# Shared-key attention in a four-layer kernel: maxima scores with 48 rows a head, two heads at once in the array's rows, and a new home for the parts of each chunk

## The reference, cut to what matters

```
q = x @ Wq            # 16 heads of 16
k, v = x @ Wk, x @ Wv # one head of 16 each, shared by all query heads
s = q k^T / 4, masked to keys at or before the query
out = softmax(s) v, heads side by side, @ Wo + bo
```

## Time and profile before

| | us |
|---|---|
| median of 3 runs (1975.9 to 1980.74) | 1979.59 |
| the profiled execution's own time | 1982.36 |
| span of its trace | 1980.3 |
| PE busy, DVE busy, ACT busy, POOL busy | 1726.5, 1056.2, 754.8, 472.2 |
| units' reductions, line 1154 (x320) | 329.9 |
| exponentials, line 1040 (x640) | 318.0 |
| scores, line 917 (x640) | 209.5 |
| units' matmuls, line 892 (x640) | 184.1 |

### The profile page before, as it was taken

The page is one execution under the profiler, slowest core; times in us unless marked ns, Lnnn a source line. Parts: engine busy times, 40 slices in busy tenths (PEclk is TensorE's granted clock), DMA queues, the critical chain, the costliest instruction groups (busy, mean ns, idle before and its releaser), DMA issues.

```text
span 1980.3 us, 24253 instructions
## 1 busy us (share of the span) xinstructions
PE 1726.5 (87%) x9372; PEld 1022.2 (52%) x9372; DVE 1056.2 (53%) x1727; ACT 754.8 (38%) x1751; POOL 472.2 (24%) x474
## 2 busy tenths in 40 slices
PE   5899577889999999969997857896899999987998
PEld 3565444433343333534555433664677777773556
DVE  2666665557678776242222867242566666743222
ACT  1210023465676777621111121013666666651110
POOL 3753230110100000040000005741344444420000
PEclk9999786899999999979998978997899999997999
DMA  3000022000000000200001030000000000002000
GB/s 104 1 1 1 14 64 70 2 1 1 2 1 1 1 1 2 90 0 0 1 0 56 0 108 0 0 0 5 6 1 7 1 7 1 1 3 86 11 11 22
DMA packets 27410, 34.02 MB, mean 17 GB/s; under 512 B 5280, under 2 KB 24544, under 8 KB 26784
## 3 DMA queue, kind: packets, MB, share of 16 engines
q1 hardware_dynamic: 27296, 32.47, 5.3%
HBM read 22.86 MB, written 2.10 MB: 13 GB/s over the span
## 4 chain that ended last, share of the span: by engine, by line
PE 67%; DVE 14%; POOL 7%; issue 6%; ACT 3%; DMA 1%; SPq 1%; POOLq 0%; DVEq 0%; ACTq 0%
PE PS L930 6%; PE PS L1208 6%; PE PS L917 6%; PE PS L1214 6%; PE PS L892 5%; PE PS L1227 5%; PE PS L1994 3%; PE PS L357 3%; PE PS L1983 2%; PE PS L1961 2%; PE PS L1633 2%; POOL arena L2179 2%; DVE arena L1154 2%; PE PS L1614 2%; PE PS L967 2%
## 5 line engine op out<-in xcount | busy, mean ns | idle before, releaser
L1154 DVE TENSOR_REDUCE arena<-PS 128x1 f32<-128x1024 f32 (+7 forms) x320 | 329.9, 1060 | 136.4 <-PE PS L894 98.9
L1040 ACT ACTIVATE arena<-PS 128x512 f32<-128x512 f32 (+3 forms) x640 | 318.0, 534 | 168.6 <-PE PS L920 77.1
L917 PE MATMUL PS<-arena 99*128 99x512 bf16 (+3 forms) x640 | 209.5, 358 | 2.0 <-ACT arena L1040 1.5
L892 PE MATMUL PS<-arena 96*128 96x512 bf16 (+3 forms) x640 | 184.1, 366 | 24.7 <-DVE arena L1154 21.9
L190 POOL TENSOR_TENSOR rstd<-ve,mhalf 128x4 f32<-128x4 f32 x32 | 32.3, 1009 | 610.3 <-DVE ve L216 610.3
L930 PE MATMUL PS<-arena 128*32 128x512 f32 (+3 forms) x1280 | 155.7, 559 | 2.8 <-ACT arena L1046 1.7
L185 ACT ACTIVATE XT<-PS 128x1024 f32<-128x1024 f32 x36 | 36.8, 1024 | 313.5 <-PE PS L178 313.5
L917 PEld LDWEIGHTS PS<-arena 99*128 99x128 bf16 x640 | 61.3, 100 | 155.4 <-ACT arena L1040 112.9
L1208 PE MATMUL PS<-XT,arena 128*128 128x512 f32 x256 | 122.7, 602 | 14.9 <-DVE arena L2376 10.4
L1258 DVE TENSOR_TENSOR arena<-arena,PS 128x512 f32<-128x512 f32 x64 | 43.9, 686 | 164.3 <-PE PS L1214 164.1
L1243 ACT ACTIVATE arena<-PS 128x512 f32<-128x512 f32 x64 | 38.2, 597 | 232.7 <-PE PS L1208 232.7
(11 more groups left out here) (233 smaller groups left out, 3031.8 us busy)
## 6 DMA issues: line engine op xcount, KB each, us to landing
arena<-arena SPq DMA_DIRECT2D x55, 128.0 KB, 2.4
X<-in_L_attn_x SPq DMA_DIRECT2D x4, 512.0 KB, 5.4
arena<-in_L_attn_out_w SPq DMA_DIRECT2D x1, 2048.0 KB, 8.1
out<-X SPq DMA_DIRECT2D x4, 512.0 KB, 2.9
arena<-in_dmask SPq DMA_DIRECT2D x1, 1024.0 KB, 7.2
arena<-in_L_ffn_W_up SPq DMA_DIRECT2D x1, 1024.0 KB, 5.0
arena<-in_L_ffn_W_gate SPq DMA_DIRECT2D x1, 1024.0 KB, 7.4
arena<-in_L_ffn_W_down SPq DMA_DIRECT2D x1, 1024.0 KB, 9.0
```

The source lines that it names most:

```text
L892: last = pe.matmul(flat[:, o:o + w], q, a.KS[0:SROWS, CH * kc:CH * kc + w], start=True, stop=kc < c)
L917: last = pe.matmul(PS[:, b, lo:CH], a.KS[0:rows, P * j:P * (j + 1)], a.QS[0:rows, G1 * g + r, CH * c + lo:CH * (c + 1)], start=True, stop= ...
L1040: act.activation(a.PB[:, n % 3, r, lo:CH], PS[:, 4 + x % 3, lo:CH], ACT.Exp, scale=D0 ** -0.5).then_inc(a.e2, 1)
L1154: dve.tensor_reduce(dst, src, AX.X, ALU.max, negate=True).then_inc(a.m1, 1)
```

## The change

The maxima no longer come from six products of parts but from three (high x high, middle x high, high x middle): 48 rows (`PACK`) in place of 96. The first 48 rows of `QS` and `KS` are these three; the other 48 rows hold the rest, and the second pass still uses all 99. For every odd head the first 48 rows are copied a second time, to rows 64 to 111 of new tensors `QO` and `KO`. A unit is now always two heads with one block of keys: one matmul over rows 0 to 47 for the even head into one bank, one over rows 64 to 111 for the odd head into the next bank. The number of units (320), of matmuls (640), of mask matmuls (256) and the elements reduced are as before; in chunks 1 to 3 a unit off the diagonal has no mask matmul and one on it has two. The partial maxima are now up to four a head, combined by a reduction for groups 4 to 15.

The parts have other homes: chunk 0 over `PB`, chunk 1 in the columns of `QS` that chunk 2 will fill, chunk 2 in those of chunk 3, chunk 3 behind all else, where `AN` of chunk 0 lies too; `AN` of the later chunks lies in used columns of `QS`. So the first exp waits for the stack of chunk 0 only; the first `normed` still waits for all. SP's queue has per chunk two steps: `first_rows` (6 transfers, a wait for their landing, the copy to `QO`, 8 heads x 48 rows, and the one to `KO`) and `other_rows` (6 transfers). Their order among the maxima rows is new. The buffers of the feed-forward block that follows are moved within the arena.

```diff
-            for t in range(TPC):
-                n = P * (t + 1)
-                for h in range(0, G1, 2):
...
+                for pair in range(G1 // 2):
+                    for kc in range(c + 1):
+                        self.units.append((i, t, pair, kc, P * (t + 1) if kc == c else CH))
...
+    def first_rows(c):
+        if c >= 2:
+            sp.wait_ge(a.second_half, 16 * HALF_DMAS * c)
+        if c == 3:
+            sp.wait_ge(a.low, 2 * c + 2)
         sp.wait_ge(a.ev, 2 * c + 1)
-        if c >= 2:
-            sp.wait_ge(a.stack[c % 2], 16 * SPLIT_DMAS)
-        stack(c, a.hb, ROWS_OF_HIGH)
+        stack(c, a.hb, 0, a.first_half)
+        stack(c, a.hb, 2, a.first_half)
         sp.wait_ge(a.mid, c + 1)
-        stack(c, a.mb, ROWS_OF_MID)
-        sp.wait_ge(a.low, 2 * c + 1)
-        stack(c, a.lb, ROWS_OF_LOW)
+        stack(c, a.mb, 1, a.first_half)
+        sp.wait_ge(a.first_half, 16 * HALF_DMAS * (c + 1))
+        if c >= 1:
+            sp.wait_ge(a.odd, 16 * 2 * c)
+        cols = slice(CH * c, CH * (c + 1))
+        sp.dma_start(a.QO[ODD:ODD + PACK, :, cols], a.QS[0:PACK, 1:H:2, cols]).then_inc(a.odd, 16)
+        sp.wait_ge(a.low, 2 * c + 2)
+        sp.dma_start(a.KO[ODD:ODD + PACK, cols], a.KS[0:PACK, cols]).then_inc(a.odd, 16)
+
+    def other_rows(c):
+        if c >= 1:
+            sp.wait_ge(a.second_half, 16 * HALF_DMAS * c)
+        stack(c, a.hb, PACK + 2, a.second_half)
+        stack(c, a.mb, PACK + 1, a.second_half)
+        stack(c, a.lb, PACK, a.second_half)
...
-    stack_chunk(0)
-    stack_chunk(1)
-    stack_chunk(2)
+    first_rows(0)
+    other_rows(0)
+    first_rows(1)
     maxima_rows(0)
-    stack_chunk(3)
+    other_rows(1)
+    maxima_rows(1)
+    first_rows(2)
+    other_rows(2)
+    maxima_rows(2)
+    first_rows(3)
+    other_rows(3)
     sp.wait_ge(a.z, 1)
...
-        for e in range(nh):
-            q = a.QS[0:SROWS, G1 * g + h0 + e, CH * c + P * t:CH * c + P * (t + 1)]
-            for b in range(nkc):
...
-                last = pe.matmul(flat[:, o:o + w], q, a.KS[0:SROWS, CH * kc:CH * kc + w], start=True, stop=kc < c)
-            if kc == c:
-                last = pe.matmul(flat[:, o + n - P:o + n], k.identb[:, :], a.mqb, start=False, stop=True)
+        pe.matmul(PS[:, b, 0:n], a.QS[0:PACK, h, at], a.KS[0:PACK, keys], start=True, stop=kc < c)
+        last = pe.matmul(PS[:, b + 1, 0:n], a.QO[ODD:ODD + PACK, h // 2, at], a.KO[ODD:ODD + PACK, keys], start=True, stop=kc < c)
+        if kc == c:
+            for e in range(2):
+                last = pe.matmul(PS[:, b + e, n - P:n], k.identb[:, :], a.mqb, start=False, stop=True)
         last.then_inc(a.s1, 1)
...
         if n == 0:
-            for par in range(2):
-                act.wait_ge(a.stack[par], 16 * SPLIT_DMAS * 2)
+            act.wait_ge(a.first_half, 16 * HALF_DMAS)
+            act.wait_ge(a.second_half, 16 * HALF_DMAS)
```

More of the change, by code:

```diff
@@ L749, in l1_alloc @@
     a.KS = take([P, T], BF16)
+    a.QO = take([P, H // 2, T], BF16)
+    a.KO = take([P, T], BF16)
     a.VX = take([P, NT, 32])
-    a.AN = take([P, H // 4, T])
+    first_parts = o
     a.PB = take([P, 3, 4, CH])
-    parts_at = o - 21 * CH
-    a.hb, a.mb, a.lb = (v(parts_at + 6 * CH * i, [P, NC, 3, CH], BF16) for i in range(3))
-    a.r1 = v(parts_at + 18 * CH, [P, 3, CH])
     a.OT = take([P, 2, CH])
@@ L768, in l1_alloc @@
     a.NM = take([P, 2, TPC, G1])
-    a.MA = take([P, 2, 2, TPC, G1])
+    a.MA = take([P, 2, NC, TPC, G1])
     a.Mr = take([P, TPC, G1])
@@ L775, in l1_alloc @@
     assert o <= 41000, o
+    last_parts = o
+    words = v(0, [P, H, T // 2])
+    first = v(o, [P, H // 4, 2, CH // 2])
+    later = [words[:, H // 2:H, CH // 2 * c:CH // 2 * (c + 1)].rearrange("p (g u) n -> p g u n", u=2) for c in range(NC - 1)]
+    a.AN = [first] + later
+    in_arena = lambda at: [v(at + 3 * CH // 2 * i, [P, 3, CH], BF16) for i in range(3)]
+    in_stack = lambda c: [a.QS[:, 3 * i:3 * i + 3, CH * c:CH * (c + 1)] for i in range(3)]
+    a.hb, a.mb, a.lb = zip(in_arena(first_parts), in_stack(2), in_stack(3), in_arena(last_parts))
+    a.r1 = words[:, 9:15, CH // 2 * 3:CH // 2 * 4]
     s = k.sem
@@ L797, in l1_sp, with stack @@
         sp.dma_start(dst, src).then_inc(a.ld, 16)
[L799 to L805, removed]
+    def stack(c, part, p, done):
+        first = p // PACK * PACK
+        for m in range(KT):
+            sp.dma_start(a.QS[p:first + PACK:3, HP * m:HP * (m + 1), CH * c:CH * (c + 1)], part[c][:, m, :]).then_inc(done, 16)
+    def first_rows(c):
[3 more added lines that the diff above has]
+            sp.wait_ge(a.low, 2 * c + 2)
         sp.wait_ge(a.ev, 2 * c + 1)
-        if c >= 2:
-            sp.wait_ge(a.stack[c % 2], 16 * SPLIT_DMAS)
-        stack(c, a.hb, ROWS_OF_HIGH)
+        stack(c, a.hb, 0, a.first_half)
+        stack(c, a.hb, 2, a.first_half)
         sp.wait_ge(a.mid, c + 1)
-        stack(c, a.mb, ROWS_OF_MID)
-        sp.wait_ge(a.low, 2 * c + 1)
-        stack(c, a.lb, ROWS_OF_LOW)
+        stack(c, a.mb, 1, a.first_half)
[12 more added lines that the diff above has]
+        stack(c, a.lb, PACK, a.second_half)
     def maxima_rows(i):
@@ L831, in l1_sp @@
         sp.dma_start(a.wo[32 * r:32 * r + D0, :, :], wo[r]).then_inc(a.ldo, 16)
-    for i in range(1, NI1):
+    for i in range(3, NI1):
         maxima_rows(i)
@@ L877, in unit @@
     def unit(u):
-        i, t, h0, nh, kc0, nkc, n = P1.units[u]
+        i, t, pair, kc, n = P1.units[u]
         c, g = i // 4, i % 4
@@ L1104, in normed @@
         if i == 0:
-            for par in range(2):
-                pool.wait_ge(a.stack[par], 16 * SPLIT_DMAS * 2)
-        pool.tensor_tensor(a.AN[:, g, CH * c:CH * (c + 1)], a.OT[:, i % 2, :], a.RD[:, i % 2, :], ALU.mult).then_inc(a.an, 1)
+            pool.wait_ge(a.first_half, 16 * HALF_DMAS * NC)
+            pool.wait_ge(a.second_half, 16 * HALF_DMAS * NC)
+        halves = lambda ap: ap.rearrange("p (u n) -> p u n", u=2)
+        pool.tensor_tensor(a.AN[c][:, g, :, :], halves(a.OT[:, i % 2, :]), halves(a.RD[:, i % 2, :]), ALU.mult).then_inc(a.an, 1)
     for n in P1.steps:
@@ L1172, in l1_dve @@
             unit(u)
-            if u in P1.last_unit and P1.units[u][0] >= 8:
+            if u in P1.last_unit and P1.units[u][0] >= 4:
                 combine(P1.units[u][0])
```

93 lines of the change are left out of this document (43 added, 50 removed).

## The result

| | before | after |
|---|---|---|
| median of 4 runs each, us | 1977.74 (1974.32 to 1980.74) | 1991.6 (1988.33 to 1993.6) |
| profiled execution: time, span | 1982.36, 1980.3 | 1993.6, 1991.6 |
| granted clock, mean of the span | 0.938 | 0.933 |

The ratio is 1.0069, with an interval of 1.0045 to 1.0093: 13.9 us slower by the medians, 11.3 by the two spans. The time lies inside the outer range, 1964 to 1994, but above the forecast's own range of 1978 to 1989, and the direction is the one I gave 0.33. Most of the surplus is one stop of PE, 12.7 us long where it was 3.6, at the place that the slower rival named.

What follows compares the result with a forecast made beforehand. PE was taken to set the pace in chunks 2 and 3; pairs +3.2, first exp -0.6 and SP's queue +0.5 gave +3.1 us on the median 1979.59, so 1983 us; own range 1978 to 1989, outer 1964 to 1994.

Steps and rivals of the forecast that it cites:

- the one I gave 0.33: Whole kernel: chance that it measures slower, against 0.45 for the same and 0.22 for faster.
- the slower rival: SP's queue: late maxima rows of group 2 stall PE and chunk 3's sequence delays the first normed; 1990 us, chance 0.2.
- SP's queue: Transfers of chunks 2 and 3 between maxima rows: each sequence 10.9 us; cost +0.5 us, ends 0 and +3.
- just in time: SP's queue: chunk 3's sequence landed by 360.7 us, where the first normed, which waits for it, had started at 360.86.
- point of 1.3 us: SP's queue: slack before group 2's maxima rows; the slower rival decides from this much delay of chunk 2's sequence.
- +7: The slower rival's part for pairs: a round trip at 0.225 us, with +3 to +5 from the queue on top.
- The clock behind the stop: Slower rival, PE after late rows: the clock falls with each stall; no size given.
- The pairs' price: PE's units: -0.016 us per pair off the diagonal, +0.063 mean on it; +3.2 us in the sum.
- Round trip: PE array switching to row halves and back: 0.20 us per unit, bounds 0.185 and 0.225, paid by all 320 units.
- The two rivals with cheap pairs: PE's units: pairs without the round trip, about 1929 us, chance 0.08; round trip partly hidden, about 0.13, 1966 us, chance 0.14.
- The first exp: ACT's wait for chunk 3's stack: 11.1 us idle before it judged no prize; gain 0.6 us, at most 2.
- DVE, copies, combining: DVE: same reduced elements, combining below 0.3 us each beside PE's work, nothing; first unit's copy waits, some 3 us, hidden.

Runs made afterwards that it cites:

- e2: e1 with each unit's two matmuls over all 96 rows, one head after the other, and no copies to QO and KO; 1976.0 us, ratio 0.9987 to the kernel before.
- e5: Changed kernel, own queue order, with AN of chunk 0 in used columns of QO, so the first normed no longer waits for chunk 3's stack; 1979.94 us, ratio 1.0013.
- e1: Changed kernel with only SP's order edited: chunk 2's transfers before the first maxima rows, chunk 3's around the second; 1980.05 us, ratio 1.0008 to the kernel before.
- e4: e1 with PE's step reordered: scores 0 and 1, values, both units' pairs side by side, scores 2 and 3; 2054.74 us, ratio 1.0394 to the kernel before.
- e6: e1 with values one step later, between scores 1 and 2, and both units between scores 2 and 3; 2026.75 us, ratio 1.0237 to the kernel before.
- e8: e4's order with the values of a block one step later; 2046.13 us, ratio 1.0347 to the kernel before.
- e9: e1 with diagonal units over 96 rows, one head after the other; only the 192 off the diagonal are pairs; 1973.82 us, ratio 0.9972 to the kernel before.
- e11: e2 (no pairs, early transfers) with the copies to QO and KO made and waited for, though unread; 1976.45 us, ratio 0.9985 to the kernel before.
- e10: e1 with only the 128 diagonal units as pairs, the 192 others over 96 rows one after the other; 1985.56 us, ratio 1.0034 to the kernel before.
- e3: e1 with both matmuls of a unit in rows 0 to 47, so mode changes stay and pairing goes; 2104.89 us, ratio 1.055 to the kernel before.

## Why the prediction was right and wrong

The time lies in the outer range, and the forecast was 8.6 us too low on the median (10.8 by medians of the same group: +13.9 measured, +3.1 forecast). What holds the time in the range is the slower rival; the forecast's own range ended at 1989.

- **SP's queue: the step that failed.** The text took a sequence of 10.9 us and "+0.5 us, with 0 and +3 as the ends". Measured at the place: the sequence of chunk 2 took 15.8 us and made the next begin 5.0 us later than reckoned (353.00 against 347.96, with 1.0 us more for a landing between them); that of chunk 3 took 15.0 us, 4.1 more; its landing 0.3 more. Sum 9.4, and `normed` is 9.2 us later than before. I aimed the doubt at the issue of the copy to `QO`, and that is 0.63 us. Mis-sized were the landing ahead of the copies, 4.1 and 4.5 us in place of 1.8, and the six issues behind them, 6.41 and 5.33 us in place of 3.9. I took both from the twelve transfers of the kernel before, which had landed 2.0 us after the end of their issue (329.59 to 331.63), because the bytes are the same. The rows written are not: those were every sixth of 96, the new ones every third of 48, and it is the six to rows 0 to 47 that land late. e2 lands them nearly as late without any copy, so the copies are not the reason for that; they are the reason for the stretched issues, of which e2 has none. The upper end, +3, should have come from a sequence with landing and issues stretched, since the text itself says "just in time": with no slack, every us of doubt goes to the end.
- **The slower rival** named place, mechanism and direction, and its 1990 is near 1991.6. But its chain was wrong in one link. It had the maxima rows of group 2 late; they were issued at 351.26 and not at 347.22, and PE did not wait for them. Nor do those of group 3 matter (e5). Its "point of 1.3 us" was a decision point of the wrong wait. It had the first `normed` late by 3 to 4 us where it was 9.2, and reached 1990 with pairs at the long end of their price, +7, which did not happen. That its time is near is in part luck.
- **The clock behind the stop** (2.0 us) was in the rival as "the clock falls with each stall", without a price.
- **The pairs' price held.** Round trip 0.20 as read from f32 rows; +3.2 in the sum, 4.05 between e1 and e2; per unit, each kind alone, +0.071 and -0.014 against +0.063 and -0.016. The two rivals with cheap pairs are out. What I missed lies in the order: a sentence says that no two pairs stand together, and I did not ask in the prediction what it would cost to bring them together. e4, e6 and e8 give that answer, 2 to 4% slower.
- **The first exp** began at 330.67 us and not before 330, yet in an execution whose first turned maxima were 1.3 us later; the turn of group 1 moved by +0.5 and that of group 2 by -0.1. That is within the forecast's "0.6, at most 2". But without pairs e2 turns group 2 3.3 us earlier than the kernel before, with the clock back at full about 4 us sooner. So there was a prize in this place, from the earlier exp or the new shape of the units, and the pairs on the diagonal took most of it: from the turn of group 1 to that of group 2 are 13.1 us in the kernel before, 10.3 in e2, e9 and e11, and 12.4 to 12.5 in the kernel after, e1 and e10. The text, which said "they aren't" a prize, counted the wait and not the clock behind it.
- **DVE, copies, combining:** costed at nothing. e11 and e2 agree, so the copies cost nothing with the early queue. DVE and the combining were not varied alone; with homes, unit shapes and first exp they sum to about -2.6 us (e2 against the kernel before), where the sum had -0.6. That and the pairs' +4.05 make e1's +1.6 (interval -0.6 to +3.6): two terms were each about 1 to 2 us off, in opposite directions.

Settled by runs: the order on SP's queue costs the loss, through `normed`'s wait (e1, e5); the pairs cost 4 us (e1, e2); the six transfers land late without the copies, and the issues stretch with them (e2, e11). Open: why the transfers to rows 0 to 47 land late, what in the units or the first exp brings e2 its 3.3 us, why the pairs' prices do not add up, and why the clock stays low in e3.

## What to carry to other kernels

When a sum says "just in time", price the wait at the end of the queue and not only the queue: take landings from transfers with the same rows, bytes and neighbours as the new ones, or double them, and ask what stands behind the waiting instruction. Row packing of a K = 48 matmul pays only where the columns saved exceed the two changes of mode, by estimate from about 475 columns at full clock (0.20 / 0.216 x 512); use it for those units and not for the rest. Ask of an idle time that you remove not only what the wait costs but what clock PE has behind it. Bringing packed matmuls together in one burst saved the changes and cost more than that here, where two other engines live on PE's alternation.

## What the runs showed of the hardware

- Transfers of 128 KB within SBUF that landed 2.4 us after issue in the median, 2.6 at most, in the kernel before took 3.4 and up to 5.1 in the kernel after. Late are those to rows 0 to 47: in e2, without copies, 3.2 rising to 4.5 within six, and 2.4 to 2.5 for the six to rows 48 to 95.
- Behind a copy of 384 KB on the same queue single issues took up to 2.1 us where 0.60 is the median (2.10 in the kernel after, 2.14 in e11); without such copies the longest took 0.71 (e2).
- Two bf16 matmuls in row halves start within 0.01 us; getting in costs 0.09 us and getting out 0.10, near the 0.20 that the f32 row halves cost for both together, and a second pair directly behind costs 0.23.
- With both units in one half of the rows PE was busy 10.00 of 10 us at a clock of 0.50 (620 to 630 us, the longest execution of e3); a busy PE is no proof of a full clock.
